# Fixed places for a half's table columns, plain register words, and wide groups ahead of the blocks on VectorE

## The reference

```
xn  = layernorm(x)
h   = elu(segment_sum((xn @ W1)[src] * w, dst) + b1)
h   = elu(segment_sum((h  @ W2)[src] * w, dst) + b2)
x   = x + h
H   = gelu(layernorm(x) @ Wf + bf)                  # 1024 wide
p   = softmax(H @ Wg + bg);  e = argmax(p)          # 8 experts
out = x + p[e] * (H @ Wd[e] + bd[e])
```

## Time and profile before

| | us |
|---|---|
| median of 3 runs (5689.48 to 5714.56) | 5709.33 |
| the profiled execution | 5730.26 |
| its span | 5728.4 |

### The profile page before, as it was taken

One profiled execution on the slowest core, in us unless ns is written; L12 is line 12 of the kernel. 1 busy time (PEld: TensorE's weight loads), 2 busy tenths in 40 slices (PEclk: granted clock), 3 DMA queues, 4 the chain that ended last, 5 costly groups with the idle time before them and its releaser, 6 DMA issues.

```text
span 5728.4 us, 84531 instructions
## 1 busy us (share of the span) xinstructions
PE 3652.3 (64%) x21450; PEld 3342.0 (58%) x21451; DVE 2030.1 (35%) x6619; ACT 1139.8 (20%) x1692; POOL 3269.0 (57%) x3403
## 2 busy tenths in 40 slices
PE   3455555555545555557667667667677666676999
PEld 2454455544545555446656666666666666665888
DVE  7222322322323322223333333333333333446333
ACT  3111111111101111013222222222222222230111
POOL 5666666666666666555555555655655555633444
PEclk6666666666666666667777777777777777778999
DMA  7333333333333333223333333333333333323554
GB/s 245 93 94 96 94 97 94 96 94 97 95 95 95 96 95 96 78 81 97 105 101 102 112 109 104 114 110 106 112 106 103 107 108 109 113 88 131 180 178 155
DMA packets 248229, 627.28 MB, mean 110 GB/s; under 512 B 63397, under 2 KB 110458, under 8 KB 247490
## 3 DMA queue, kind: packets, MB, share of 16 engines
q0 software_dynamic: 170688, 492.87, 29.8%
q1 hardware_dynamic: 76930, 129.30, 6.3%
HBM read 519.25 MB, written 103.63 MB: 109 GB/s over the span
## 4 chain that ended last, share of the span: by engine, by line
PE 40%; issue 22%; DVEq 3%; DVE 3%; ACT 1%; another core or an unknown queue 1%; DMA 0%; POOL 0%; ACTq 0%; POOLq 0%; SPq 0%
PE pB L1228 13%; PE pA L1187 13%; PE pA L1314 6%; PE pC L1210 3%; PE pZ L1197 2%; DVE S L862 1%; DVEq L862 1%; PE pC L1304 1%; PE pB L1304 1%; PE pZ L1221 1%; DVEq L890 0%; PE pT L1238 0%; PE pT L1216 0%; DVEq L903 0%
## 5 line engine op out<-in xcount | busy, mean ns | idle before, releaser
L1187 PE MATMUL pA<-S,rows 128*128 128x96 f32 x12544 | 1877.1, 314 | 1124.4 <-issue 786.0
L1187 PEld LDWEIGHTS pA<-S,rows 128*128 128x128 f32 x12544 | 1815.7, 230 | 1211.2 <-issue 881.6
L541 POOL DMA_INDIRECT rows<-h_scratch,idx x1568 | 1499.7, 956 | 1194.1 <-PE pA L1187 506.6
L541 POOL DMA_INDIRECT rows<-xn_scratch,idx x1568 | 1493.9, 953 | 832.2 <-issue 438.4
L1228 PE MATMUL pB<-work,w 128*128 128x128 f32 x3232 | 780.6, 374 | 738.6 <-issue 731.1
L1228 PEld LDWEIGHTS pB<-work,w 128*128 128x128 f32 x3232 | 644.9, 272 | 865.2 <-issue 863.9
L862 DVE TENSOR_SCALAR S<-iota_p,tdst,twgt 128x96 f32<-128x96 f32 x3168 | 888.4, 344 | 311.2 <-issue 294.8
L903 DVE TENSOR_TENSOR aggT<-aggT,pA 128x192 f32 x784 | 275.1, 351 | 1762.1 <-remote 907.7
L634 ACT ACT_TABLE_LOAD x196 | 251.5, 1283 | 1874.2 <-DVE aggT L903 883.8
L912 DVE TENSOR_TENSOR zb<-pZ,brow 128x256 f32<-128x256 f32 x198 | 84.0, 424 | 951.7 <-issue 556.9
L666 ACT ACTIVATE work<-pC 128x768 f32<-128x768 f32 x103 | 83.5, 811 | 1615.9 <-remote 1558.9
(11 more groups left out here) (177 smaller groups left out, 2158.3 us busy)
## 6 DMA issues: line engine op xcount, KB each, us to landing
pay_scratch<-work SPq DMA_DIRECT2D x98, 512.0 KB
rows<-xn_scratch,idx POOLq DMA_INDIRECT x1568
rows<-h_scratch,idx POOLq DMA_INDIRECT x1568
h_scratch<-work SPq DMA_DIRECT2D x98, 128.0 KB
pay_scratch<-work SPq DMA_DIRECT2D x98, 128.0 KB
work<-in_x_dram SPq DMA_DIRECT2D x97, 128.0 KB
rows<-in_x_dram SPq DMA_DIRECT2D x24, 512.0 KB, 5.7
xn_scratch<-rows SPq DMA_DIRECT2D x24, 512.0 KB, 6.3
```

The source lines that it names most:

```text
L541: pool.indirect_dma_start(rows[:, s, t, :], None, source, bass.IndirectOffsetOnAxis(at, 0))\
L1187: last = mm(to[:, k * W:(k + 1) * W], rows[:, slot, t, k * P:(k + 1) * P], Sx[:, t, :], start=(t == 0), stop=(t == T - 1))
```

## The change

Tables: `tdst` and `twgt` become one table `tdw` that keeps, for each group, four targets and four weights side by side. At the end of a half VectorE copies the columns of the half two later into `cols`, one of two fixed places (`stage_cols`, 32 elements of each partition). `S` and `Sov` read their scalars from there, at places known when the program is built. A new semaphore `s_cols` counts the copies; a half waits on it ahead of its edges.

Register words: `regs` has 8 words for each half, each plain: the flag, first tick, end of ticks, four first targets. VectorE loads seven of them by one call at the start of the half, TensorE three, ScalarE two; nothing is shifted or masked, and nothing is loaded inside the edges.

Order on VectorE: both adds of a pair come first, then the eight `S` instructions of the pair. `build_S` no longer waits for TensorE on its own. A half with overflow does its edges ahead of the ticks, one without after them, by two tests instead of one test with an else. TensorE waits once a pair, for the matrices of both groups.

Small ones: `zeros` is one column that is broadcast; `etab` lies in `regs`; a step that waits for VectorE's own adds is a plain wait (`wait_ge`) and no longer also a step of a semaphore (`hold`).

```diff
-        tdst = sb("tdst", [P, T, TBL])
-        twgt = sb("twgt", [P, T, TBL])
-        tsrc = sb("tsrc", [P, T, TBL], i16)
+        tdw = sb("tdw", [P, TBL, 2, T])
+        tsrc = sb("tsrc", [P, TBL, T], i16)
+        cols = sb("cols", [P, 2, HALF, 2, T])
-        regs = sb("regs", [1, NH + 1, 4], i32)
+        regs = sb("regs", [1, NH + 1, 8], i32)
...
+        def half_regs(eng, h, first, last):
+            _, values = nc.values_load_multi_w_load_instructions(
+                regs[0:1, bass.ds(h, 1), first:last].rearrange("a h r -> a (h r)"), engines=[eng.engine],
+                min_val=0, max_val=N - 1, skip_runtime_bounds_check_because=
+                "flags, numbers of blocks and dsts are below the number of nodes")
+            return values
         def half_flags(eng, h):
-            v = eng.value_load(regs[0:1, bass.ds(h, 1), 0], min_val=0, max_val=(1 << 17) - 1)
-            return v >> 16, (v >> 8) & 255, v & 255
+            return half_regs(eng, h, 0, 3)
...
-            def build_S(layer, g, half):
-                dve.wait_ge(s_mm[layer], g + (SLOTS - HALF + 1))
-                for t in range(T):
-                    last = v.tensor_scalar(S[:, half, t, :], iota_w[:, :], tdst[:, t, bass.ds(g, 1)],
-                                           twgt[:, t, bass.ds(g, 1)], ALU.is_equal, ALU.mult)
-                last.then_inc(s_S[layer], 1)
+            def stage_cols(layer, h, half):
+                v.tensor_copy(cols[:, half, :, :, :].rearrange("p g a t -> p (g a t)"),
+                              tdw[:, bass.ds(h * HALF, HALF), :, :].rearrange("p g a t -> p (g a t)"))\
+                 .then_inc(s_cols[layer], 1)
+            def build_S(layer, g, half, u):
+                for n in (u, u + 1):
+                    for t in range(T):
+                        last = v.tensor_scalar(S[:, n, t, :], iota_w[:, :], cols[:, half, n, 0, t:t + 1],
+                                               cols[:, half, n, 1, t:t + 1], ALU.is_equal, ALU.mult)
+                    last.then_inc(s_S[layer], 1)
...
-            def edges_half(layer, h, with_overflow):
+            def edges_half(layer, h, half, bases, with_overflow):
+                dve.wait_ge(s_cols[layer], h + 2)
                 for u in range(0, HALF, 2):
                     g = HALF * h + u
-                    pair = dve.value_load(regs[0:1, bass.ds(h, 1), 1 + u // 2], min_val=0,
-                                          max_val=(1 << 2 * PACK) - 1)
-                    bases = ...
...
                     dve.wait_ge(s_mm[layer], g + 2 + SLOTS)
                     for n in range(2):
-                        hold(dve, s_add[layer], g + n + HALF)
-                        to = aggT[:, :, bass.ds(bases[n], W)]
+                        dve.wait_ge(s_add[layer], g + n + HALF)
+                        to = aggT[:, :, bass.ds(bases[u + n], W)]
                         v.tensor_tensor(to, to, group_sum(u + n)..., ALU.add).then_inc(s_add[layer], 1)
-                        build_S(layer, g + n + HALF, u + n)
+                    build_S(layer, g + HALF, 1 - half, u)
...
-                        ovf, start, end = half_flags(dve, h)
+                        ovf, start, end, *bases = half_regs(dve, h, 0, 3 + HALF)
+                        with dve.If(ovf > 0):
+                            edges_half(layer, h, half, bases, True)
                         ticks(dve, start, end, (tick1, tick2)[layer])
-                        with dve.If(ovf > 0):
-                            edges_half(layer, h, True)
-                        with dve.Else():
-                            edges_half(layer, h, False)
+                        with dve.If(ovf < 1):
+                            edges_half(layer, h, half, bases, False)
+                        stage_cols(layer, h + 2, half)
                         stage_idx(layer, h + AHEAD, (i & 1) * 2 + half)
...
-                    pe.wait_ge(s_S[layer], g + 1)
                     if u % 2 == 0:
+                        pe.wait_ge(s_S[layer], g + 2)
                         pe.wait_ge(s_add[layer], g + 2)
```

More of the change, by code:

```diff
@@ L84, in bass_gnn_then_routed_ffn @@
     EPS = 1e-5
-    PACK = 14
     KWIN = (N - 1) // W
@@ L91, in bass_gnn_then_routed_ffn @@
     assert NH - 1 + LEAD >= NB
-    assert SLOTS == 2 * HALF and HALF == 4 and NB < 256 and NPAD < (1 << PACK)
+    assert SLOTS == 2 * HALF and HALF == 4
     assert NB % (2 * LB) == 0 and C + (KH - FUSED) * P <= 512 and 0 < TAILG <= 32 and FULL_ROWS > BODY
@@ L258, in bass_gnn_then_routed_ffn @@
         s_gath = [[sem(f"rows_gathered_{l}_{i}") for i in range(SLOTS)] for l in range(2)]
+        s_cols = [sem(f"table_columns_staged_{l}") for l in range(2)]
         s_S = [sem(f"S_ready_{l}") for l in range(2)]
@@ L680, in _ @@
                         h = 2 * i + half
-                        _, start, end = half_flags(act, h)
+                        start, end = half_regs(act, h, 1, 3)
                         ticks(act, start, end, lambda j: (tick1, tick2)[layer](j, h))
-                _, start, end = half_flags(act, NH)
+                start, end = half_regs(act, NH, 1, 3)
                 ticks(act, start, end, lambda j: (tick1, tick2)[layer](j, NH))
@@ L810, in _ @@
                 tc.then(v.tensor_copy(wins[0:1, :, r], frm[:, 0:NG]))
[L811 to L815, removed]
+            tc.then(v.memset(regs[0:1, NH:NH + 1, :], 0))
+            tc.then(v.tensor_copy(regs[0:1, 0:NH, 3:3 + HALF], LOr[:, 0:NG].rearrange("o (h g) -> o h g", g=HALF)))
             A, B, R = grow(5), grow(6), grow(7, i32)
-            FL, FLX = grow(2)[:, 0:NH], grow(2)[:, 0:NH + 1]
+            FL = grow(2)[:, 0:NH]
             tc.then(v.memset(work[0:1, 5 * GCH * P:7 * GCH * P], -float(P)))
@@ L835, in _ @@
             tc.then(v.tensor_tensor(FL, INC4[:, :, HALF - 1], STA4[:, :, 0], ALU.subtract))
[L836 to L841, removed]
+            tc.then(v.tensor_scalar(regs[0:1, 0:NH, 0], FL, 1.0, None, ALU.min))
+            tc.then(v.memset(regs[0:1, 0:2, 1], 0))
+            tc.then(v.memset(regs[0:1, 0:1, 2], 0))
+            tc.then(v.tensor_copy(regs[0:1, 1:NH + 1, 2], A[:, 0:NH]))
+            tc.then(v.tensor_copy(regs[0:1, 2:NH + 1, 1], A[:, 0:NH - 1]))
             tc.then(v.memset(work[:, :], 0.0))
@@ L853, in _, with overflow @@
             dve.wait_ge(s_tcopied, 3 * GCH)
-            dve.wait_ge(s_tbl_clear, 3)
+            dve.wait_ge(s_tbl_clear, 2)
             dve.wait_ge(s_regs, 1)
             dve.wait_ge(s_aggclear, 2)
-            def build_S(layer, g, half):
-                dve.wait_ge(s_mm[layer], g + (SLOTS - HALF + 1))
-                for t in range(T):
-                    last = v.tensor_scalar(S[:, half, t, :], iota_w[:, :], tdst[:, t, bass.ds(g, 1)],
-                                           twgt[:, t, bass.ds(g, 1)], ALU.is_equal, ALU.mult)
-                last.then_inc(s_S[layer], 1)
-            def overflow(layer, g, base):
+            def stage_cols(layer, h, half):
[8 more added lines that the diff above has]
+                    last.then_inc(s_S[layer], 1)
+            def overflow(layer, g, half, u, base):
                 ws, we = overflow_windows(dve, g)
@@ L897, in edges_half @@
                         for n in range(2):
[L898 removed]
+                            overflow(layer, g + n, half, u + n, bases[u + n])
                     dve.wait_ge(s_mm[layer], g + 2 + SLOTS)
                     for n in range(2):
[L901 to L902 removed]
+                        dve.wait_ge(s_add[layer], g + n + HALF)
+                        to = aggT[:, :, bass.ds(bases[u + n], W)]
                         v.tensor_tensor(to, to, group_sum(u + n).rearrange("p (k n) -> p k n", k=KC), ALU.add)\
                          .then_inc(s_add[layer], 1)
[L905 removed]
+                    build_S(layer, g + HALF, 1 - half, u)
             def z_biased(layer, j):
@@ L986, in _ @@
                 dve.sem_inc(s_add[layer], HALF)
-                for u in range(HALF):
-                    build_S(layer, u, u)
+                for half in range(2):
+                    stage_cols(layer, half, half)
+                dve.wait_ge(s_cols[layer], 1)
+                dve.wait_ge(s_mm[layer], SLOTS)
+                for u in range(0, HALF, 2):
+                    build_S(layer, u, 0, u)
                 with dve.Fori(0, ITERS) as i:
```

28 lines of the change are left out of this document (12 added, 16 removed).

## The result

The changed kernel takes 5806.95 us (median of 4 runs, 5797.73 to 5813.7) against 5699.4 for the kernel before beside it: ratio 1.019, 95% interval 1.015 to 1.022. It is slower, by 1.5 to 2.2%. The forecast was 5485, and the time is outside the range. The profiled execution took 5802.72 us with a span of 5801.0 (before: 5730.26 and 5728.4).

The account below looks back on a forecast made before the run. The prediction took VectorE to bound layer 1 and TensorE layer 2. Savings of 165 us in layer 1 and 60 in layer 2 made 225: 5505 us profiled, x 0.9963 = 5485 us, range 5330 to 5710.

Parts of the forecast that it names:

- VectorE bounds layer 1: In layer 1 VectorE's instructions and their issue are late in the chain of waits; the edge products have 1.5%.
- three quarters of what it saves stay: Layer 1: of 2.2 us a half off VectorE, 1.7 us is kept, as GpSimd's shorter pauses slow more remaining instructions.
- forecast 165 us: Layer 1's kept saving, 1.7 us x 98; bounds 0 and 350, the latter GpSimd's floor.
- a sign of being wrong: The prediction is wrong if layer 1 keeps 23 us a half with fewer register operations.
- the stretches take it back: Rival: GpSimd gathers sooner, dispatch is slow for longer, and the half keeps its length; 5700 us, chance 0.15.
- Layer 2 gains 60 us because TensorE's slow stretch shares its rate with VectorE: Layer 2: fewer VectorE instructions in slow stretches, 0.18 us each, give 0.65 us a half, 60 us; bounds 0 and 245.
- Waiting for the whole pair: TensorE waits for both groups' S: taken as 0 on the end; bounds -1 and +1.07 us a pair.
- The rival's 5810 us: Rival: TensorE starts each pair 1.07 us later and GpSimd pauses as much longer; 5810 us, chance 0.12.
- The jump moves ahead of the tick: VectorE's stall at the overflow code's jump moves ahead of L912; layer 1: 0, bounds -2 and +1 us a half.
- The load of seven words costs 0.3 us more: VectorE's load of flags carries seven words: one further trip, 0.3 us more; bounds 0 and 1.8 us.
- The copy of 0.2 us: VectorE's stage_cols copy behind the edges: 0.2 us a half, bounds 0.15 and 0.5.
- The 78 us: By the Trainium skill's page the seven-word load is 0.8 us a half dearer than taken, the sum 78 us smaller.

Follow-up runs that it names:

- e8: e1 with three of the four weighting matrices of every group left out in layer 1; 5521 us, 0.962 of the kernel before.
- e1: e0 with six small GpSimd memsets ahead of the fourth group's gathers of every half in layer 2; 5506 us, 0.964 of the kernel before.
- e9: e0 with GpSimd waiting, ahead of the fourth group's gathers in layer 2, until the third group's have landed; 5496 us, 0.957 of the kernel before.
- e0: The control: the changed kernel with one bound on a loaded register word (two register operations a load); 5918 us, 1.038 of the kernel before.
- e7: The kernel before with the memsets of e1 ahead of the fourth group's gathers in layer 2; 5584 us, 0.976 of the kernel before.
- e2: e0 with three of the four weighting matrices of every group left out in layer 2; 5986 us, 1.048 of the kernel before.
- e4: e0 with a one-element memset ahead of each S in layer 2, 16 VectorE instructions more a half; 5689 us, 0.991 of the kernel before.
- e5: e0 without the column copy and its wait, S reading its columns from the table at a register's place; 5754 us, 1.004 of the kernel before.
- e6: e0 with the ticks first and both forms of the edges behind them as If and Else; 5951 us, 1.041 of the kernel before.
- e3: e0 with the old order in a pair (add, its S, add, its S), TensorE waiting for each group's S alone; 5942 us, 1.041 of the kernel before.
- e11: e0 with three memsets ahead of the second and three ahead of the fourth group's gathers in layer 2; 5397 us, 0.940 of the kernel before.
- e13: e11 with its gaps of three memsets in layer 1 too; 5399 us, 0.939 of the kernel before.
- e14: e13 with gaps of two memsets in place of three; 5497 us, 0.957 of the kernel before.

## Why the prediction was wrong

- **VectorE bounds layer 1, and three quarters of what it saves stay: wrong.** The saving on VectorE was real (idle of issue ahead of `S` and the adds fell by 632 us in layer 1), and so was TensorE's wait for its adds, 285.4 us, which is gone. But the layer kept 7 of the forecast 165 us. TensorE's idle of issue grew by 332 us in place of that wait, and the half kept its 23.6 us, which the prediction had named as a sign of being wrong. So VectorE was late, but the next limit stood 0.1 us a half behind it. With VectorE off the chain nothing more is to be had from it: in e8 12 instructions fewer a half gain nothing. The rival "the stretches take it back" was right for layer 1; the size of the three quarters had no row behind it.
- **Layer 2 gains 60 us because TensorE's slow stretch shares its rate with VectorE: wrong in sign.** Layer 2 lost 87 us where 60 were to be gained, 147 us of the miss, beside layer 1's 158. The earlier trace rows do show that TensorE issues faster while VectorE stands still. I took the stretch's length as given, and that is the step that failed. In the changed kernel TensorE's step comes through before GpSimd asks in 42 halves, where it was 19; GpSimd then does not stop, and the stretch goes on to the end of 16 gathers, at 3.9 us a half. The pause that I would have called a loss (the earlier trace rows count it so in layer 1) was what let TensorE work. e1 and e9 put pauses back and gain 412 and 422 us against the control, and with the pause in both kernels the change is no loss but a gain (e7). Why the change raised the share is less sure. That fewer of VectorE's instructions let the step through sooner fits e2 (90 long halves, the control 70), e4 and e5 (21 and 30); e4 and e5 moved the instruction queue's transfers too, and e0 and e6 do not fit. So it is supported, not shown.
- **Waiting for the whole pair costs nothing: right.** TensorE's idle for `S` in layer 2 is 3.7 us and e3 changes nothing. The rival's 5810 us is within 0.1% of the measured time by another cause.
- **The jump moves ahead of the tick: half right.** The idle ahead of the adds went, but did not come back ahead of the bias, where idle of issue in layer 1 fell from 427.8 to 229.7 us. In e6 its place is worth nothing in time.
- **The load of seven words costs 0.3 us more: too little, within its bounds.** Columns: minimum, median, maximum in ns.

```profile
L363 ACTq TENSOR_LOAD <-regs x198: 481/490/1086, 113.2 to 5179.6; - x198
L363 PEldq TENSOR_LOAD <-regs x198: 766/772/1770, 113.7 to 5194.4; - x198
L363 DVEq TENSOR_LOAD <-regs x198: 700/1044/2017, 116.6 to 5197.6; - x198
```

One word took VectorE 0.295 us; two take ScalarE 0.49, three TensorE 0.77, seven VectorE 1.04 in the median: 0.75 us more. VectorE has under 1% of the chain in the stretches shown, so nothing there shows the load's own length as what made the kernel slower. The Trainium skill ("Runtime: NRT & Kernel Launch", Instruction fetch mechanics) has about 200 ns for each register, in bulk too, an estimated 1.4 us: two and three words come to 245 and 257 ns a word, seven to 149, so the row lies under its rule at seven. The 78 us that the prediction takes off by that page leave out its own three quarters; with them it is 59.
- **The copy of 0.2 us: right**, 179 ns, as the index copy's.

```profile
L863 DVE COPY cols<-tdw 128x32 f32 x196 | 35.0, 179 | 0.0
```

Not settled: what in the slow stretch delays the step; why the control's two register operations raise the share from 42 to 70 where sixteen elsewhere lower it; whether VectorE's instructions act by their number, by their time, or by the instruction queue's transfers. The load of seven words was not undone by itself.

## What to carry to other kernels

Where one engine's stream slows the others, look at how the stretches follow its runs before crediting a saving: if the step that ends a run's pause comes sooner, the run grows longer, and that can cost more than was saved. A pause in the profile may be doing work; put one in and see. When only a rhythm's share changes, count its two kinds from the trace, and in more than one execution: the chain of waits in layer 2 looked alike before and after. Here two short gaps for GpSimd in each half of layer 2 (e11) give 5397 us, 0.940 of the kernel before, with the change kept.

## What was not expected of the hardware

While gathers go out one every 1.26 us, semaphore steps of other engines arrive late: TensorE's products end 4.6 us after the half's start in the long half shown and 5.2 us in the short one, and VectorE's adds, which wait for their step, begin 13.9 and 17.4 us after it. A gap of 3.8 us from one gather to the next ends that, and so does one of 2.9 us after only eight gathers. In layer 1 the pauses add up to 3.2 or 3.3 us a half over the sixteen gathers' 20.1 whether they come as one (e1), as two (e13) or as more (e14); why this sum is constant stays open.
